# Routed experts in 128-slot blocks from a bf16 copy of the weights in DRAM, each expert loaded once

## The chip, the cores and the metric

The kernel runs on all 8 cores of one Trainium2 chip. Every core works on one sequence of the batch and on its own copy of the inputs; nothing is exchanged. The metric is the device time of the slowest core in microseconds (us).

## The reference, cut to what matters

```python
x = x + attention(layernorm(x), Wq, Wk, Wv)       # causal, one head of width 1024; x: (8, 2048, 1024)
h = layernorm(x)
shared = (silu(h @ shared_gate.T) * (h @ shared_up.T)) @ shared_down.T    # inner width 2048
probs = sigmoid(h @ router_w.T)                    # 8 experts
scores, indices = top_k(probs, 2); scores /= scores.sum(-1)
w[t, e] = the score of token t for expert e, zero elsewhere
routed = sum_e w[:, e] * ((silu(h @ gate_w[e]) * (h @ up_w[e])) @ down_w[e])
x = x + shared + routed
```

One expert is 3 x 1024 x 2048 = 6.29 million weights, f32 in DRAM. A core has 2048 tokens and so 4096 pairs of token and expert. With the reference's inputs the pairs spread evenly: on every core each expert gets between 448 and 577 of them.

## The kernel before

It is written by hand for the five engines, each with its own program (`sync_program`, `gpsimd_program`, `tensor_program`, `vector_program`, `scalar_program`), ordered by semaphores. PE is TensorE, DVE VectorE, ACT ScalarE, POOL GpSimd, SP the engine that only issues DMAs and waits. Names that begin with `t_`, `s_`, `v_` are semaphores that TensorE, ScalarE and VectorE raise.

**Attention.** `x` goes into `R2` (f32, all 2048 tokens). Layernorm, transposes into `XQ` (feature by token), then K, V and Q from `wk`, `wv`, `wq`, which POOL loads with a cast from f32 to bf16 (only POOL's DMAs cast here); `wq` waits for the last K product. Causal scores, softmax and weighted values run tile by tile (16 query tiles of 128). The second layernorm's rows go to the DRAM tensor `x2` and, transposed, to `XQ`.

**Routing.** L506 gives the logits. The DVE program then runs `route_choose` (the two largest per token) ahead of its first product, and `route_place` after product 4. Every instruction of these goes through `chain`, which raises `v_rt` and waits for it. `tri` and `ones` are 128x128 constants for two small matmuls that turn the choice into ranks. 32 indirect DMAs write token and score of each slot to the table `tab` in DRAM, which comes back as `tabS`.

**Shared expert.** Two halves of 1024 tokens. `unit` computes 128 inner features of 512 tokens: 8 matmuls 128x512 for gate (L515), 8 for up (L519), with the weights as stationary and the tokens as moving operand, so the product is already feature by token. ScalarE takes the silu (L895), VectorE multiplies (L748). `down` then makes 16 matmuls per 128 tokens and 512 columns (L527). POOL streams the weights with the cast.

**Routed experts.** Slots are sorted by expert and each expert's share is padded to blocks of `BS` = 512: `NBLK` = (2*2048 + 8*511)//512 = 15 blocks, always all of them. A block loads its expert's weights whole, f32 to bf16 (8 gate/up groups of 1 MB bf16, in the six `slots`, and 4 parts of `dw`, into `VBUF` or a part of `R2` by turns), though neighbouring blocks mostly have the same expert. `gather_block` fetches 4 x 128 rows of `x2`, `transpose_block` (L539) turns them, then 16 units, then 8 `down` of 16 matmuls. VectorE scales by the score (L782) and POOL adds the rows to `out` in DRAM with an indirect, accumulating DMA (L388), one per 128 rows.

Of the kernel before, what the change touches and what calls it, by code (L numbers as in the profile page):

```python
# [7 lines left out]
I32 = mybir.dt.int32  # L8
AF = mybir.ActivationFunctionType
# [11 lines left out]
BS = 512  # L21
NBLK = (2 * S + NE * (BS - 1)) // BS
SUB = BS // 128
NSUB = NBLK * SUB
NSLOT = NBLK * BS
NKB = S // BS
NC_L8, NC_L16, NC_KB, NC_BI = 0, 64, 320, 320 + NKB
NCONST = NC_BI + NBLK
RT_SEL, RT_SLOT, RT_ALL = 12, 36, 39
# [12 lines left out]
def build_program():  # L42
# [6 lines left out]
    sgu_d = nc.dram_tensor("sgu", [8, 128, 4096], F32, kind="ExternalInput").ap()  # L49
    sdw_d = nc.dram_tensor("sdw", [4, 128, 4096], F32, kind="ExternalInput").ap()  # L50
    gu_d = [nc.dram_tensor("gu%d" % g, [NE, 128, 4096], F32, kind="ExternalInput").ap()
            for g in range(8)]
    dw_d = [nc.dram_tensor("dw%d" % k, [NE, 128, 4096], F32, kind="ExternalInput").ap()
            for k in range(4)]
# [13 lines left out]
    R2 = nc.alloc_sbuf_tensor("R2", [128, NTT, D], F32)  # L68
    XQ = nc.alloc_sbuf_tensor("XQ", [128, NHC, S], BF16)
    KBUF = nc.alloc_sbuf_tensor("KBUF", [128, 16384], BF16)  # L70
    VBUF = nc.alloc_sbuf_tensor("VBUF", [128, 16384], BF16)
    WBUF = nc.alloc_sbuf_tensor("WBUF", [128, 8192], BF16)
    sS = nc.alloc_sbuf_tensor("sS", [128, 5760], BF16)
    sP = nc.alloc_sbuf_tensor("sP", [128, 2, S], BF16)
    sPT = nc.alloc_sbuf_tensor("sPT", [128, 8, 128], BF16)
    xlntm = nc.alloc_sbuf_tensor("xlntm", [128, 2, D], BF16)
    gscr = nc.alloc_sbuf_tensor("gscr", [128, 2, 512], BF16)
    ident = nc.alloc_sbuf_tensor("identsb", [128, 128], BF16)
    dmask = nc.alloc_sbuf_tensor("dmasksb", [128, 128], BF16)
    rwTs = nc.alloc_sbuf_tensor("rwTs", [128, NHC, NE], BF16)  # L80
    rbias = nc.alloc_sbuf_tensor("rbiassb", [128, NE], F32)
    lgt = nc.alloc_sbuf_tensor("lgt", [128, NTT, NE], F32)
    prb = nc.alloc_sbuf_tensor("prb", [128, NTT, NE], F32)
    sel = nc.alloc_sbuf_tensor("sel", [128, NTT * NE], BF16)
# [78 lines left out]
    init_done = sem("init_done")  # L163
    sc_done = sem("sc_done")
    tab_in = sem("tab_in")
    g_in = sem("g_in")
    out_init = sem("out_init")
    add_done = sem("add_done")

# [823 lines left out]
```

## Time and profile before

| | us |
|---|---|
| median of 3 runs (lowest, highest) | 2572.2 (2489.29, 2572.78) |
| the profiled execution | 2511.08 |
| its span on the slowest core, which is core 1 | 2509.5 |
| spans of the eight cores | 2470.6 to 2509.5 |

All rows are of that one execution and, where nothing else is said, of core 1. A window row gives, for a stretch in us from the span's start, the busy time of each engine with its count of instructions, then the clock that the throttle granted TensorE as a share of full speed, the mean busy share of the core's 16 DMA engines (short windows can show a little over 1), and the GB/s that they moved, counted at the destination. A cast from f32 to bf16 thus reads twice the GB/s shown.

### The profile page before, as it was taken

The page shows a single profiled execution, that of the slowest core. Times are in us where ns is not written, and L with a number is a line of the kernel's source. Part 1 is how long each engine was busy: PE and PEld are TensorE (multiplying, and loading weights), DVE is VectorE, ACT ScalarE, POOL GpSimd, SP SyncE. Part 2 cuts the span into 40 slices and gives each one's busy share as a digit, 9 for nine tenths or more (in the row PEclk, how much of TensorE's full clock was granted, in tenths as well). Part 3 has the DMA queues.
Part 4 walks back from the last instruction along what each step waited for, and adds up shares of the span by engine and source line. Part 5 has one row for each costly group of instructions (what it writes and reads, how often), then busy time and mean ns, then how long its engine had stood idle before and what let it go on. Part 6 is the DMA issues. An engine that isn't in the chain of part 4 may idle for free.

```text
span 2509.5 us, 26342 instructions; the slowest of 8 cores (2470.6 to 2509.5 us)
## 1 busy us (share of the span) xinstructions
PE 2057.3 (82%) x9914; PEld 959.9 (38%) x9914; DVE 471.4 (19%) x757; ACT 457.2 (18%) x856; POOL 301.4 (12%) x366
## 2 busy tenths in 40 slices
PE   0689766755899999897897977979779798797898
PEld 0335633332334444343343433434334343343343
DVE  3100143324111112121111211112112111121111
ACT  4333434431100110111101111011111120111100
POOL 1000000002300000020120201202112022020111
PEclk9789978877888899998998989989889898898999
DMA  9010100002951456989989889898898998988985
GB/s 215 2 24 11 34 22 17 14 20 30 108 74 59 77 86 146 175 138 151 159 142 172 139 152 164 143 172 144 138 179 143 161 153 138 178 145 152 164 139 96
DMA packets 62826, 287.11 MB, mean 114 GB/s; under 512 B 16192, under 2 KB 16320, under 8 KB 37072
## 3 DMA queue, kind: packets, MB, share of 16 engines
q0 software_dynamic: 47936, 263.63, 63.7%
q1 hardware_dynamic: 14768, 21.80, 2.7%
q8 instruction: 83, 1.36, 0.2%
q14 instruction: 39, 0.32, 0.0%
HBM read 457.72 MB, written 44.92 MB: 200 GB/s over the span
## 4 chain that ended last, share of the span: by engine, by line
PE 60%; DMA 28%; issue 4%; DVE 4%; ACT 2%; POOL 0%; DVEq 0%; ACTq 0%; POOLq 0%
PE psE L527 12%; DMA VBUF<-dw 12%; DMA R<-dw 12%; PE psF L527 11%; PE psA L515 7%; PE psC L519 6%; PE psD L519 6%; PE psB L515 6%; DMA WBUF<-sgu 2%; DMA WBUF<-wk 2%; PE psC L443 2%; PE psD L443 1%; DVE R L638 1%; PE psA L459 1%; PE psA L416 1%
## 5 line engine op out<-in xcount | busy, mean ns | idle before, releaser
L895 ACT ACTIVATE gscr<-psA 128x512 bf16<-128x512 f32 x152 | 90.8, 597 | 1183.6 <-PE psA L515 1183.5
L527 PE MATMUL psE<-VBUF,KBUF 128*128 128x512 bf16 x768 | 195.6, 413 | 97.6 <-DMA VBUF<-dw 95.4
L527 PE MATMUL psE<-R,KBUF 128*128 128x512 bf16 x448 | 116.7, 420 | 94.7 <-DMA R<-dw 94.7
L388 POOL DMA_INDIRECT out<-R,tabS x60 | 95.1, 1585 | 786.1 <-DVE R L782 468.7
L748 DVE TENSOR_TENSOR KBUF<-gscr,psC 128x512 bf16<-128x512 bf16 x152 | 104.5, 688 | 451.6 <-PE psC L519 416.9
L748 DVE TENSOR_TENSOR KBUF<-gscr,psD 128x512 bf16<-128x512 bf16 x152 | 104.5, 688 | 436.4 <-PE psD L519 415.6
L527 PE MATMUL psF<-VBUF,KBUF 128*128 128x512 bf16 x768 | 179.7, 389 | 0.0
L895 ACT ACTIVATE gscr<-psB 128x512 bf16<-128x512 f32 x152 | 90.8, 597 | 453.3 <-PE psB L515 435.1
L527 PEld LDWEIGHTS psE<-VBUF,KBUF 128*128 128x128 bf16 x768 | 79.7, 105 | 204.5 <-issue 140.0
L782 DVE TENSOR_SCALAR R<-psE,tabS 128x512 f32<-128x512 f32 x60 | 45.1, 751 | 432.9 <-PE psE L527 432.9
L527 PEld LDWEIGHTS psF<-VBUF,KBUF 128*128 128x128 bf16 x768 | 76.6, 100 | 95.2 <-issue 19.7
L515 PE MATMUL psA<-XQ,WBUF 128*128 128x512 bf16 x256 | 76.1, 452 | 39.2 <-DMA WBUF<-sgu 26.4
L527 PEld LDWEIGHTS psE<-R,KBUF 128*128 128x128 bf16 x448 | 47.0, 106 | 158.7 <-issue 116.2
L527 PE MATMUL psF<-R,KBUF 128*128 128x512 bf16 x448 | 101.3, 379 | 0.0
L402 PE MATMUL psG<-identsb,xlntm 128*128 128x128 bf16 x64 | 11.0, 267 | 96.2 <-DMA WBUF<-wk 54.2
L360 POOL DMA_DIRECT2D XQ<-gu x80 | 49.6, 619 | 305.5 <-PE psD L519 297.9
L519 PE MATMUL psC<-sS,XQ 128*128 128x512 bf16 x336 | 79.4, 379 | 0.0
L515 PE MATMUL psA<-sS,XQ 128*128 128x512 bf16 x336 | 79.4, 379 | 0.0
L519 PE MATMUL psD<-sS,XQ 128*128 128x512 bf16 x336 | 79.4, 379 | 0.0
L515 PE MATMUL psB<-sS,XQ 128*128 128x512 bf16 x336 | 79.4, 379 | 0.0
L443 PE MATMUL psC<-VBUF,sPT 128*128 128x512 bf16 x136 | 60.6, 446 | 21.0 <-ACT sPT L832 21.0
L782 DVE TENSOR_SCALAR R<-psF,tabS 128x512 f32<-128x512 f32 x60 | 45.1, 751 | 161.4 <-PE psF L527 161.4
(209 smaller groups left out, 2643.1 us busy)
## 6 DMA issues: line engine op xcount, KB each, us to landing
XQ<-gu POOLq DMA_DIRECT2D x80, 1024.0 KB, 37.5
WBUF<-gu POOLq DMA_DIRECT2D x40, 1024.0 KB, 37.6
VBUF<-dw POOLq DMA_DIRECT2D x32, 1024.0 KB
R<-dw POOLq DMA_DIRECT2D x28, 1024.0 KB, 33.0
WBUF<-sgu POOLq DMA_DIRECT2D x16, 1024.0 KB, 10.4
R<-x SPq DMA_DIRECT2D x4, 2048.0 KB, 24.0
out<-R SPq DMA_DIRECT2D x16, 512.0 KB, 2.6
x<-xlntm SPq DMA_DIRECT2D x16, 256.0 KB, 2.0
```

What stands on the lines that cost most here:

```text
L360: eng.dma_start(out=halves(slots[r % 6]), in_=halves(src)).then_inc(w_in[r % 6], 16)
L388: eng.indirect_dma_start(out=out_d, out_offset=bass.IndirectOffsetOnAxis(ap=tabS[:, q, 0:1], axis=0), in_=y[:, q % 4, :], in_offset=None, ...
L416: mm = eng.matmul(b[:, 0:w], XQ[:, ec, qi * 128:(qi + 1) * 128], kfm[:, ec, ks * 512:ks * 512 + w], start=(ec == 0), stop=(ec == NHC - 1))
L443: mm = eng.matmul((psC, psD)[eh][:, :], sPT[:, kc % 8, :], vtm[:, kc, eh * 512:(eh + 1) * 512], start=(kc == 0), stop=(kc == qi))
L459: mm = eng.matmul(pj[g % 4][:, :], wqkv[:, d, ec * 128:(ec + 1) * 128], XQ[:, d, ts * 512:(ts + 1) * 512], start=(d == 0), stop=(d == NHC ...
L515: mm = eng.matmul((psA, psB)[u % 2][:, :], w[:, 0, hc, ic * 128:(ic + 1) * 128], moving[:, hc, :], start=(hc == 0), stop=(hc == NHC - 1))
L519: mm = eng.matmul((psC, psD)[u % 2][:, :], w[:, 1, hc, ic * 128:(ic + 1) * 128], moving[:, hc, :], start=(hc == 0), stop=(hc == NHC - 1))
L527: mm = eng.matmul((psE, psF)[n % 2][:, :], a[:, i, tt * 128:(tt + 1) * 128], w[:, i, hh * 512:(hh + 1) * 512], start=(i == 0), stop=(i == ...
L638: eng.scalar_tensor_tensor(R2[:, qi, eh * 512:(eh + 1) * 512], (psC, psD)[eh][:, :], qst[:, 3, qi:qi + 1], R2[:, qi, eh * 512:(eh + 1) * 512],
L748: eng.tensor_tensor(dst, gscr[:, u % 2, :], (psC, psD)[u % 2][:, :], op=ALU.mult).then_inc(v_mul, 1)
L782: eng.tensor_scalar(y[:, q % 4, hh * 512:(hh + 1) * 512], (psE, psF)[n % 2][:, :], tabS[:, q, 1:2].bitcast(F32), None, op0=ALU.mult).then_ ...
L895: eng.activation(gscr[:, u % 2, :], (psA, psB)[u % 2][:, :], AF.Silu).then_inc(s_silu, 1)
```

## The change

**Weights.** The host packs each expert (the shared one is number 8) into 8 chunks of [128, 6144] f32: 256 columns of gate, the same 256 of up, and the 256 rows of down that belong to them. 72 POOL DMAs without a wait between them cast all nine experts, DRAM to DRAM, into `wb` (bf16). SP, whose DMAs can't cast, then loads chunks of `wb` into `wring`, two buffers of one expert each (98,304 bytes per partition and buffer). The whole of SBUF is one tensor `arena`; attention's tensors lie where the ring will be.

**Blocks.** `BS` = 128, so `NBLK` = (4096 + 8*127)//128 = 39 blocks, always all of them. From the reference's inputs 34 to 37 of them are filled on a core, and each expert has 4 or 5. VectorE computes for each block which buffer holds its expert (`pints`) and which load, if any, follows it (`lints`). A load that isn't needed is skipped by a condition on the DMA. A load for the next expert goes out when the last block of the one before has left the buffer, and the first expert's waits for all casts.

**Steps.** Shared and routed work have one form: 55 tiles of 128 tokens (16 shared, 39 routed), 8 steps each. Step k: `gate_up` (8 matmuls 128x512, tokens stationary, weights moving), `transpose_h` of step k-2 (2 transposes), `down` of step k-3 (4 matmuls 128x512). ScalarE takes the silu of 256 columns and copies the transposed product, VectorE multiplies 256 columns.

```diff
-BS = 512
+NCH = 8
+CH = 6144
+BS = 128
@@ gpsimd_program
         eng.wait_ge(t_kv, 32)
         eng.dma_start(out=wqkv[:, :, :],
                       in_=wq_d.rearrange("(c p) e -> p c e", p=128)).then_inc(wq_in, 16)
-        load_shared(0, 0)
-        load_shared(0, 1)
+        for e in [NE] + list(range(NE)):
+            for c in range(NCH):
+                eng.dma_start(out=wb_d[c][e, :, :], in_=w_d[c][e, :, :]
+                              ).then_inc(cast_done[0 if e == NE else 1], 16)
+
+        eng.wait_ge(t_pt, pair_no["p", NTT - 1, n_pairs(NTT - 1) - 1] + 1)
+        eng.dma_start(out=tri, in_=tri_d).then_inc(tri_in, 16)
         eng.wait_ge(v_rt, RT_SLOT)
@@ sync_program
+        def before_first(c):
+            if c == 0:
+                eng.wait_ge(cast_done[1], 16 * NCH * NE)
+            if c == 5:
+                store_out(NTT - 1)
+                eng.wait_ge(t_gu, NCH * NTT)
+            elif c < 5:
+                for tt in range(3 * c, 3 * c + 3):
+                    store_out(tt)
...
+        load_expert(0, before_first)
+        load_expert(1, lambda c: eng.wait_ge(t_dn, NCH * (NTT - 1) + c + 1))
+        for blk in range(NBLK - 2):
+            load_expert(blk + 2, lambda c: eng.wait_ge(t_dn, NCH * (NTT + blk) + c + 1))
@@ tensor_program
+        def moving(k, off, use):
+            tile, c = k // NCH, k % NCH
+            if tile < NTT:
+                return use(wring[:, 0, c, off:off + 512])
+            v = bass.RuntimeValue.of_register_unchecked(base[tile - NTT], min_val=0,
+                                                        max_val=B1 // 2) * 2
+            at_byte = 2 * (c * CH + off)
+            mm = use(arena[:, bass.ds(v + at_byte, 1024)].bitcast(BF16))
...
+        for k in range(NSTEP + 3):
+            if k < NSTEP:
+                gate_up(k)
+            if 2 <= k < NSTEP + 2:
+                transpose_h(k - 2)
+            if k >= 3:
+                down(k - 3)
+            if k == 4:
+                eng.wait_ge(v_rt, RT_SEL)
+                eng.matmul(psH[:, 0:128], tri, sel, start=True, stop=True)
+                eng.matmul(psH[:, 128:256], ones, sel, start=True, stop=True).then_inc(t_rk, 1)
+            if k == NCH:
+                eng.wait_ge(v_rt, RT_ALL)
+                eng.load(base[0:20], pints[0:1, 0:20])
+                eng.load(base[20:NBLK], pints[0:1, 20:NBLK])
@@ vector_program
         def route_choose():
             eng.wait_ge(s_sig, 1)
-            eng.wait_ge(init_done, 48)
+            eng.wait_ge(rc_in, 32)
+            eng.wait_ge(tri_in, 16)
+            chain(eng.memset(ones, 1.0))
...
+        route_choose()
+        for k in range(NSTEP + 3):
+            if k < NSTEP:
+                product(k)
+            if k % NCH == 2 and k > NCH:
+                evacuate(k // NCH - 1)
+            if k == 5:
+                route_place()
+                route_blocks()
```

In `gate_up`, step k waits for product k-3 (`v_mul`), since three PSUM banks take turns. The routing is 77 chained instructions in place of 39.

Where instructions move, shown at three places (in the rows `arena` is any tensor of the change in SBUF, and what stands in brackets is what the instruction waits for).

POOL's program before, from the constants to the first writes of the table: `tri` comes early, and behind `wq` come two groups of the shared expert.

```order
L312 DMA trisb<-tri 128x128
L313 DMA WBUF<-wk 128x8x1024
L315 DMA sS<-wv 128x4x1024
L317 DMA sP<-wv 128x4x1024
L319 DMA x<-zero 16x8192
L321 DMA WBUF<-wq 128x8x1024 [waits t_kv]
L288 DMA WBUF<-sgu 128x4096 [waits t_q] x2
L293 DMA tab<-tabsb,slot 7680x2 [waits v_rt,init_done]
L293 DMA tab<-tabsb,slot 7680x2 x5
```

POOL's program in the change, from `wv` to the first gather: the 72 casts stand behind `wq` with no wait of their own, and `tri`, the 32 writes of the table and the gathers now stand behind the casts.

```order
L389 DMA arena<-wv 128x4x1024
L391 DMA arena<-wv 128x4x1024
L393 DMA x<-zero 16x8192
L395 DMA arena<-wq 128x8x1024 [waits t_kv]
L399 DMA wb<-w 48x16384 x72
L403 DMA arena<-tri 128x128 [waits t_pt]
L408 DMA tab<-arena 4992x2 [waits v_rt,init_done]
L408 DMA tab<-arena 4992x2 x31
L377 DMA arena<-x,arena 128x1024 [waits v_rt,tab_in,x2_out,pad_done]
```

Moved: `tri` from the first constants to behind the last cast; new: 226 MB read and 113 MB written in one run of POOL's queue.

VectorE before, the start of `route_choose`: it waits for `s_sig` and for constants that SP loads on its own queue.

```order
L692 TENSOR_REDUCE rst<-prb 128x16 [waits s_sig,init_done]
L693 TENSOR_TENSOR KBUF<-prb,rst 128x128 [waits v_rt]
L684 TENSOR_TENSOR KBUF<-KBUF 128x1024 [waits v_rt]
L686 TENSOR_REDUCE KBUF<-KBUF 128x128 [waits v_rt]
L687 SCALAR_TENSOR_TENSOR KBUF<-KBUF 128x128 [waits v_rt]
L696 SCALAR_TENSOR_TENSOR KBUF<-KBUF,prb 128x128 [waits v_rt]
```

VectorE in the change, the same place: the first instruction waits for `tri_in` too. 18 more of the chain follow without another engine's semaphore, then product 0 (L830).

```order
L750 MEMSET arena 128x128 [waits s_sig,rc_in,tri_in]
L739 TENSOR_REDUCE arena<-arena 128x16 [waits v_rt]
L740 TENSOR_TENSOR arena<-arena 128x128 [waits v_rt]
L741 TENSOR_TENSOR arena<-arena 128x128 [waits v_rt]
L742 TENSOR_REDUCE arena<-arena 128x16 [waits v_rt]
L743 TENSOR_TENSOR arena<-arena 128x128 [waits v_rt]
```

Moved: the constants' load is now waited for from POOL's queue as well; the products stand behind the routing as before.

TensorE before, the start of a routed block: 8 gate and 8 up matmuls per unit, with addresses fixed in the program.

```order
L515 MATMUL psA<-sS,WBUF 128x512 [waits s_x,w_in0,s_silu,v_mul]
L515 MATMUL psA<-sS,WBUF 128x512 x7
L519 MATMUL psC<-sS,WBUF 128x512 x8
L515 MATMUL psB<-sS,WBUF 128x512 [waits s_silu,v_mul]
L515 MATMUL psB<-sS,WBUF 128x512 x7
L519 MATMUL psD<-sS,WBUF 128x512 x8
L515 MATMUL psA<-sS,WBUF 128x512 [waits w_in1,s_silu,v_mul]
L515 MATMUL psA<-sS,WBUF 128x512 x7
```

TensorE in the change, in a routed block, from the `transpose_h` of one step to the first `gate_up` matmul of the next: each 128x512 matmul on the ring has an instruction ahead of it that computes its address in a register.

```order
L585 MATMUL psF<-arena 128x128 [waits v_mul,s_ht]
L585 MATMUL psF<-arena 128x128
L600 REGISTER_ALU [waits s_ht]
L600 MATMUL psD<-arena 128x512
L600 REGISTER_ALU
L600 MATMUL psE<-arena 128x512
L600 REGISTER_ALU
L600 MATMUL psD<-arena 128x512
L600 REGISTER_ALU
L600 MATMUL psE<-arena 128x512
L576 REGISTER_ALU [waits we_in1_1,v_mul]
L576 MATMUL psC<-arena 128x512
```

What moved: gate and up are one accumulation of 512 columns, the down products stand among them, and the 3,744 matmuls 5,280 such matmuls the 3,744 of the routed blocks have that instruction; the 1,536 of the shared expert have none.

## Rows read from the trace of the kernel before

**Rows 1.** The page's 40 slices: busy tenths of TensorE and of the DMA engines.

```profile
PE   0689766755899999897897977979779798797898
...
DMA  9010100002951456989989889898898998988985
```

**Rows 2.** Windows of the stages: attention, shared expert, routed blocks.

```profile
302.00:566.00 264.00, 174.99 (x958) 84.75 (x956) 95.03 (x206) 98.84 (x256) 0.00 (x0) 0.80 0.07 22
566.00:984.00 418.00, 376.01 (x1569) 161.26 (x1570) 84.75 (x136) 44.87 (x71) 48.37 (x60) 0.88 0.52 82
984.00:2510.00 1526.00, 1308.64 (x6218) 597.47 (x6216) 255.84 (x361) 196.25 (x296) 244.64 (x290) 0.92 0.89 151
```

**Rows 3.** The chain that ended last: start us, us, what.

```profile
1014.92 36.83 DMA VBUF<-dw
1052.10 6.38 PE psE L527 x16
1058.48 3.45 PE psF L527 x16
...
1111.44 44.39 DMA R<-dw
```

**Rows 4.** A window inside a block, between accumulating DMAs.

```profile
1114.00:1144.00 30.00, 26.01 (x143) 12.56 (x141) 5.41 (x8) 7.96 (x11) 2.12 (x4) 0.98 1.01 169
```

**Rows 5.** Windows of core 0: its first shared-expert load, from 292 us.

```profile
296.00:298.00 2.00, 2.00 (x14) 1.54 (x12) 0.58 (x2) 0.00 (x0) 0.00 (x0) 0.50 1.09 229
...
300.00:302.00 2.00, 1.28 (x7) 0.62 (x7) 1.16 (x4) 1.07 (x5) 0.00 (x0) 0.88 0.98 172
```

**Rows 6.** Windows of core 1, the same load, from 295 us.

```profile
300.00:302.00 2.00, 2.00 (x10) 1.15 (x9) 0.87 (x4) 0.00 (x0) 0.00 (x0) 0.50 1.00 176
...
306.00:308.00 2.00, 0.77 (x5) 0.14 (x3) 1.89 (x3) 0.00 (x0) 0.00 (x0) 1.00 1.00 205
```

**Rows 7.** Timeline of POOL: start us, us, engine line op out<-in.

```profile
175.59 0.93 POOL L321 DMA_DIRECT2D WBUF<-wq  x1 [167.79 <-PE psD L459]
```

**Rows 8.** DMA issues: out<-in engine op xcount, KB, us to landing.

```profile
XQ<-gu POOLq DMA_DIRECT2D x80, 1024.0 KB, 37.5
...
out<-R SPq DMA_DIRECT2D x16, 512.0 KB, 2.6
...
WBUF<-wq POOLq DMA_DIRECT2D x1, 2048.0 KB, 17.2
...
sP<-wv POOLq DMA_DIRECT2D x1, 1024.0 KB, 58.7
...
x<-zero POOLq DMA_DIRECT2D x1, 256.0 KB, 59.3
```

**Rows 9.** Line 360, POOL's sequencer: min/median/max ns.

```profile
L360 POOLq ALU_OP  x30: 32/32/49, 913.6 to 2335.6; - x30
```

**Rows 10.** Line 349, a register loaded from SBUF: min/median/max ns.

```profile
L349 POOLq TENSOR_LOAD <-eblki x15: 285/291/498, 900.3 to 905.0; - x15
```

**Rows 11.** Timeline of TensorE: the transposes of a block.

```profile
1137.74 0.61 PE L539 MATMUL psG<-identsb,sP 128*128 128x128 bf16 x8
1138.19 0.61 PE L539 MATMUL psH<-identsb,sP 128*128 128x128 bf16 x8
```

**Rows 12.** Timeline of VectorE: two neighbours of the routing's chain.

```profile
572.71 0.29 DVE L696 SCALAR_TENSOR_TENSOR KBUF<-KBUF,prb 128x128 f32<-128x128 f32 x1
573.10 0.29 DVE L698 TENSOR_REDUCE rst<-KBUF 128x16 f32<-128x128 f32 x1
```

**Rows 13.** Core 1 in the shared expert's first `down`.

```profile
735.00:800.00 65.00, 63.99 (x245) 26.37 (x244) 10.32 (x15) 0.10 (x1) 0.53 (x1) 0.81 0.24 73
```

**Rows 14.** Core 2 in the same stretch.

```profile
735.00:800.00 65.00, 65.00 (x302) 29.45 (x301) 13.07 (x19) 2.32 (x4) 0.00 (x0) 1.00 0.22 74
```

**Rows 15.** The page's costliest groups: ScalarE's silu.

```profile
L895 ACT ACTIVATE gscr<-psA 128x512 bf16<-128x512 f32 x152 | 90.8, 597 | 1183.6 <-PE psA L515 1183.5
```

**Rows 16.** Timeline of POOL: the last accumulating DMA.

```profile
2501.14 1.55 POOL L388 DMA_INDIRECT out<-R,tabS  x1 [5.35 <-DVE R L782]
```

More of the change, by code:

```diff
@@ L1 @@
+import math
 import numpy as np
@@ new lines, in build_program @@
+    slot = in_u(2 * NTT).bitcast(I32).rearrange("p (k a) -> p k a", k=2)
+    bt1, bt2 = [in_u(NBLK * NE).rearrange("p (b e) -> p b e", b=NBLK) for _ in range(2)]
+    bev = in_u(2 * NBLK * 4).rearrange("p (b e) -> p b e", e=4)
+    od, kk, fl, le, nx = [in_u(NBLK) for _ in range(5)]
+    par = in_u(2 * NBLK)
+    pev = in_u(2 * NBLK)
+    e8 = rconst[:, NC_E8:NC_E8 + NE]
+    eid = rconst[:, NC_ID:NC_ID + NE]
+    l8 = rconst[:, NC_L8:NC_L8 + 64].rearrange("p (a b) -> p a b", a=NE)
+    kbs = rconst[:, NC_KB:NC_KB + NKB]
@@ L311, in gpsimd_program @@
                       in_=rwT_d.rearrange("(c p) e -> p c e", p=128)).then_inc(c_in, 16)
-        eng.dma_start(out=tri[:, :], in_=tri_d).then_inc(c_in, 16)
         eng.dma_start(out=wqkv[:, :, :],
@@ new lines, in gate_up @@
+        def gate_up(k):
+            tile, c = k // NCH, k % NCH
+            blk = tile - NTT
+            if tile == 0:
+                eng.wait_ge(ws_in[c], 16)
+            elif blk >= 0:
+                if c == 0:
+                    eng.wait_ge(s_x, blk + 1)
+                eng.wait_ge(we_in[blk % 2][c], 16 * (blk // 2 + 1))
+            if k >= 3:
+                eng.wait_ge(v_mul, k - 2)
+            for hc in range(NHC):
+                x = XQ[:, hc, tile * 128:(tile + 1) * 128] if blk < 0 else xT[:, blk % 2, hc, :]
+                mm = moving(k, hc * 512, lambda w: eng.matmul(
+                    psGU[k % 3][:, :], x, w, start=(hc == 0), stop=(hc == NHC - 1)))
+            mm.then_inc(t_gu, 1)
@@ new lines, in transpose_h, with down @@
+        def transpose_h(k):
+            eng.wait_ge(v_mul, k + 1)
+            if k >= 1:
+                eng.wait_ge(s_ht, k)
+            for j in range(2):
+                mm = eng.transpose(hps[:, k % 2, j * 128:(j + 1) * 128],
+                                   sil[:, k % 3, j * 128:(j + 1) * 128], ident[:, :])
+            mm.then_inc(t_ht, 1)
+        def down(k):
+            tile, c = k // NCH, k % NCH
+            eng.wait_ge(s_ht, k + 1)
+            if c == 0 and tile == 0:
+                eng.wait_ge(v_lg, 1)
+            if c == 0 and tile >= 1:
+                eng.wait_ge(v_y, y_written(tile - 1))
+                if tile > NTT:
+                    eng.wait_ge(s_y, tile - NTT)
+            for j in range(2):
+                for hh in range(2):
+                    mm = moving(k, 4096 + j * 1024 + hh * 512, lambda w: eng.matmul(
+                        psY[hh][:, :], hT[:, k % 2, j * 128:(j + 1) * 128], w,
+                        start=(c == 0 and j == 0), stop=(c == NCH - 1 and j == 1)))
+            if tile >= NTT and c == NCH - 1:
+                v = bass.RuntimeValue.of_register_unchecked(base[tile - NTT], min_val=0,
+                                                            max_val=B1 // 2)
+                eng.free_register(eng.lower_val(v * 2))
+                eng.free_register(base[tile - NTT])
+            mm.then_inc(t_dn, 1)
```

696 lines of the change are left out of this document (322 added, 374 removed).

## The prediction

> **What bounds the kernel now.** I read the page's 40 slices first [rows 1]. TensorE is busy everywhere, but from the sixteenth slice on the DMA engines are at 8 or 9 tenths as well, so the busy share alone doesn't say which of them sets the pace. The windows by stage [rows 2] give the sizes: attention ends near 566 us, the shared expert takes 418 us, the 15 routed blocks 1526 us, that is 101.7 us each, with the DMA share at 0.89. The chain of waits [rows 3] decides it. In every block a stretch of 37 to 44 us belongs to the landing of the down weights, and only the last part of the block to TensorE's 3.45 us per 16 matmuls. A block computes 384 matmuls of 512 columns at 3.45/16 = 0.216 us, which is 83 us; its weights are 25.2 MB of f32, and at the 169 GB/s (338 GB/s read) of a window of weight loads alone [rows 4] they take 74 us, to which gathers and additions come. So the routed stage stands between two limits, and the loads decide its last wait. TensorE's 5,760 routed matmuls (1242 us) lie close under it.
>
> **What the change takes away.** 39 blocks of 128 slots hold 4,992 slots, where 15 of 512 hold 7,680. The matmuls per slot stay the same, so 3,744 are left, 2,016 fewer: 435 us of TensorE at 0.216. Added are 2 transposes in each of the 440 steps (55 tiles x 8); the 8 transposes per 128 slots go from 480 to 312. Eight transposes start 0.45 us after the eight before them [rows 11], 0.056 each. Each expert has 4 or 5 blocks of about 22 us, so its successor's 12.6 MB have 88 us or more to arrive, and at 338 GB/s they need 37. The waits of [rows 3] therefore go in the routed stage.
>
> **When the casts end.** This carries the forecast. POOL issues `wq` at 175.6 us [rows 7], and it lands 17.2 us later [rows 8], at 193. The casts follow in the same queue with no wait. Nine experts of 6.29 million weights are 226.5 MB read and 113.2 MB written, all in DRAM; in the same time SP stores `x2` (4.2 MB) and reads the shared copy (12.6 MB). Sum 356.5 MB. What rate? Two cores show that they share the memory. Core 0 loads at 229 GB/s while core 1 hasn't begun, and at 172 when both load [rows 5]; core 1 has 176 then, and 205 once core 0 is done [rows 6]. Since the cast reads twice what it writes, both together take some 340 GB/s each from DRAM, the same as [rows 4]. No row has reads and writes of DRAM mixed at full rate. One bound counts only reads (239 MB at 338: 707 us, casts end at 900). The other counts all bytes and takes a tenth off for the mixing (1172 us, end at 1365). I take all bytes at 338, because what two cores compete for is the memory, and the writes go to it as well: 1055 us, end at 1248.
>
> The Trainium skill, HBM Reference, Specifications, gives about 358 GB/s per core when both cores of a pair run. The trace is 6% under it. By that figure the casts would end at 193 + 996 = 1189 and the sum below would be 59 us lower.
>
> **Who waits for the casts.** The first expert's load does, by its own wait. But `tri`, 32 KB, stands behind the 72 casts in POOL's queue too. That the queue is served in order shows in the landings: a load of 1 MB, which takes 6 us alone at 169 GB/s, lands 37.5 us after its issue when others stand ahead, and `x` from `zero`, issued behind `wv`, lands last [rows 8]. VectorE's `route_choose` waits for `tri` ahead of product 0, and step 3 waits for product 0. So TensorE finishes attention at about 566 us, does three `gate_up`, and stands until 1250. All attention work is under this cover, with any delay that the casts cause in the `x2` stores: it would have to last 680 us to cost anything. If the cover is gone, the shared expert runs beside the casts (rival below).
>
> The Trainium skill, DMA: Bandwidth & Descriptors, Queues, rings and completion order, says that each engine takes a ring's descriptors in ring order; by this `tri` can't overtake. It also says that an engine goes round between the queues, so an SP load of `tri` would have passed. The rows agree with the first.
>
> **From the casts' end to the end.**
> - Landing of `tri`, 2 us (like 2.6 for a store [rows 8]). 19 chained instructions, 13 of them 0.39 apart [rows 12], 6 shorter, near 0.3: 7 us. A start at the lower of the clock's two levels, 2 us.
> - After product 5, 58 chained instructions at about 0.3: 17.4 us. TensorE has three steps of its own meanwhile (8 us), so 9 us are exposed.
> - At step 8 TensorE loads 39 registers. One costs 0.29 us on POOL [rows 10]; two instructions fetch them all, so the cost lies between 0.6 and 11.3 us; I take 6.
> - 440 steps of 12 x 0.216 + 2 x 0.056 = 2.70 us: 1188 us; 312 transposes of rows, 17 us; less three `gate_up` done before, 5 us. Beside it, in a step, ScalarE has one silu of half the 512 columns that take 0.60 us [rows 15] and one copy, so it fits.
> - The address instruction ahead of each matmul: 32 ns on POOL's sequencer [rows 9]. A transpose with its weight load passes in 56 ns, and 56 + 32 is far below 216: nothing. That is the bound from below; a matmul with a register's address has no row, and if it took the spacing to 0.27 it would cost 200 us.
> - First expert: its chunk 5 lies on `R2` and may load only when tile 15 is stored. Evacuation 1.5, store 2.6 [rows 8], landing about 7: 11 us against the 5 that two steps cover. Chunks 6 and 7 come at 4.7 us against steps of 2.7. Together 10 us.
> - Last addition: as now 8 to 10 us from its issue [rows 16]; 10.
>
> Sum: 1248 + 11 + 9 + 6 + 1200 + 10 + 10 = 2494 us at the full clock.
>
> **The clock.** TensorE works 1200 us without a gap on all cores. Before, while all cores computed densely, core 2 was granted 1.00 and core 1 only 0.81 for the same 65 us [rows 13, 14]. At 0.81 a step takes 2.70/0.81 = 3.33 us, 0.63 more. The slowest core counts; between never and always I take a sixth of the steps at 0.81, nearer to core 2's row since the clock was 0.92 on core 1 over the whole routed stage with its rests [rows 2], +46 us, bounds 0 and 100 for the likeliest case. **Forecast 2540 us**, 1% over the profiled execution's 2511, which lies between the lowest (2489) and the median (2572) of the runs shown.
>
> **Rivals.**
> 1. *Writes cost the memory nothing.* The casts end at 900, 348 us earlier: about 2190 us. For it: one core alone read at 458 GB/s [rows 5], so its DMA engines are not the limit. Against it: the competition of two cores. Chance 12%.
> 2. *`tri` doesn't wait for the casts*, so the change does what it is meant to: the shared expert runs from 566 to about 940 in their cover, and only the routed blocks follow the casts. 1248 + 39 x 22.1 + 15 for first loads + 10 + the clock's 30: 2165 us. Against it the order of landings. Chance 8%.
> 3. *TensorE is slowed as soon as it is dense* (slower). Nothing now lets it rest for 1200 us. At 0.81 throughout: 2494 + 440 x 0.63 = 2771 us; it decides against the forecast from about half the steps on. For it core 1's rows, against it core 2's. Chance 12%. The Trainium skill, TensorE: Matmul & The Clock Gate, The HAM clock gate, says that dense matmuls on three cores of a die take the whole die to 13/16 of the clock. That is this rival. The trace agrees with the level (0.81) and not with the reach: core 2 of the same die kept 1.00.
> 4. *Register addresses slow the matmuls* (slower): 2540 + 200 = 2740. Chance 4%.
>
> **How the numbers follow.** The likeliest case has 64%. Its own range is 2435 (casts by the smaller figure's 59 us less, full clock) to 2700 (mixing costs a tenth, +117, and clock +100). A change of 2% is about what a measurement of this kernel can tell from none; against 2489 to 2511 that is below about 2450, or above about 2555. Of the 64, I put 8 below, 28 within and 28 above. With rivals 1 and 2 (20) below and 3 and 4 (16) above: faster 0.28, same 0.28, slower 0.44. The range from 2165 to 2740 leaves out most of rival 1 and the upper half of rivals 3 and 4.
>
> **What would show it.** A DMA share near 1 from 193 us to the casts' end, with about 108 GB/s of bf16 written; `tri` landing at 1248; TensorE idle from 570 until then; steps of 2.70 us behind it with no wait for weights except in the first routed block. Wrong would be the forecast if TensorE starts the shared expert before 600 us, if the casts end before 1150, or if a step takes over 3 us.

## The result and the profile after

The changed kernel took 2569.85 us (median of four runs, lowest 2567.4), the kernel before on the same chip 2541.11 (median of four). The ratio is 1.028, 95% interval [1.020, 1.035]: slower by nearly 3%. It isn't the quotient of the two medians: it compares 2489.3 and 2510.0 us before with 2567.4 to 2570.0 after, since two of the four runs before (2572.8 and 2572.2), one of the changed kernel (2741.47, with one die's mean granted clock at 0.76 to 0.80 and not 0.82) and such runs of the experiments below (five of the six with `tri` early) were in a slower state, and what is said of the clock holds for the others alone. The profiled execution of the changed kernel took 2567.4 us, on its slowest core, 6, a span of 2565.6. The result lies inside the range, but the forecast of 2540 lay 1.3% under the median of 2572.2 that was shown before it and 1.2% over the profiled 2511, so it called no clear change where there is one.

First the page's slices of the changed kernel, beside [rows 1].

```profile
PE   0689722233343010000149999959999999999997
...
PEclk9789966566666555555569999989999999999999
DMA  9029999999999999999702111182774572735111
GB/s 210 1 32 117 110 130 115 113 115 114 116 115 114 114 133 140 112 138 132 108 9 59 50 49 51 44 293 45 226 214 130 153 228 44 235 89 184 39 38 26
```

The two engines have changed places. From slice 4 to slice 19 the DMA engines are full. TensorE falls to 2 to 4 tenths from slice 6 and to nearly nothing from slice 14. From slice 22 it is full, but for one slice, and the DMA engines rest between bursts. The routed stage lost the weight waits of [rows 3] as intended, and what the casts cost before it was added in front. The windows of core 6 (columns as in [rows 2]) give the sizes.

```profile
315.00:900.00 585.00, 156.79 (x776) 75.49 (x788) 82.79 (x170) 94.20 (x242) 0.59 (x1) 0.64 1.00 117
...
1190.00:1250.00 60.00, 0.00 (x0) 0.00 (x0) 0.00 (x0) 0.00 (x0) 0.00 (x0) 0.50 1.00 117
1272.00:1342.00 70.00, 30.97 (x128) 13.10 (x132) 20.12 (x72) 6.53 (x19) 31.03 (x32) 0.67 0.03 8
1342.00:1670.00 328.00, 326.26 (x1668) 156.11 (x1700) 69.84 (x150) 79.26 (x243) 1.95 (x2) 1.00 0.14 51
1670.00:1720.00 50.00, 26.82 (x128) 12.21 (x129) 4.54 (x10) 8.14 (x20) 3.56 (x3) 0.89 0.96 308
1720.00:2557.00 837.00, 825.73 (x4403) 402.63 (x4490) 154.41 (x337) 257.29 (x674) 95.00 (x73) 1.00 0.45 129
```

While only casts ran, 117 GB/s were written, and the read side moves twice that. Behind 1342 the clock is 1.00 except around the first routed blocks (0.89 in the window from 1670), and of the last 837 us TensorE is busy for 826. The wait itself, in VectorE's timeline and then in TensorE's, each with the idle time and its releaser in brackets:

```profile
1265.18 0.17 DVE L750 MEMSET arena<- 128x128 bf16 x1 [346.64 <-DMA arena<-tri]
```

```profile
1272.67 0.37 PE L585 MATMUL psF<-arena 128*128 128x128 bf16 x2 [278.76 <-DVE arena L830]
```

VectorE stood 347 us for `tri` and ran `route_choose` in 7.5. The landings of the small transfers say why (engine, size, us to landing).

```profile
arena<-rconst SPq DMA_DIRECT2D x1, 69.5 KB, 148.8
arena<-tri POOLq DMA_DIRECT2D x1, 32.0 KB, 446.9
arena<-tokid SPq DMA_DIRECT2D x1, 8.0 KB, 180.7
```

```profile
x<-arena SPq DMA_DIRECT2D x16, 256.0 KB, 40.3
```

That is the page's median of the 16 stores of `x2`: 40 us each beside the casts, where a store of twice its size took 2.6 before [rows 8]. The 181 us of `tokid` (8 KB) are not its own price alone, since it stands behind three chunks of the shared expert and `rconst` in SP's queue; it lands 32 us after `rconst`. That stretched attention from 566 us to 918, in the cover of the casts. Last, the waits that are left from 1260 us on (us in total, times, longest), in which the first row is the wait for `tri`.

```profile
PE psF L585 <- DVE arena L830: 278.8, 1, 278.8
PE psF L585 <- ACT arena L970: 21.0, 1, 21.0
PE psB L576 <- DMA arena<-wb: 14.5, 4, 8.4
PE psF L585 <- issue: 14.4, 1, 14.4
PE psA L576 <- DMA arena<-wb: 6.1, 3, 3.0
PE psC L576 <- DMA arena<-wb: 4.9, 3, 2.6
PE psA L576 <- issue: 1.8, 1, 1.8
```

### The profile page after: what moved, and what is told of

Same layout as the page of the kernel before. It is cut to its first block, busy times and chain, and to the rows that moved or that the text cites. A ratio compares the mean times of both kernels' runs of the same rounds, so it can differ in the third digit from the quotient of the medians.

```text
span 2565.6 us, 31247 instructions; the slowest of 8 cores (2536.8 to 2565.6 us)
## 1 busy us (share of the span) xinstructions
PE 1586.1 (62%) x8455; PEld 786.9 (31%) x8610; DVE 382.4 (15%) x834; ACT 571.1 (22%) x1450; POOL 175.7 (7%) x196
## 3 DMA queue, kind: packets, MB, share of 16 engines
q0 software_dynamic: 19040, 150.63, 47.6%
q1 hardware_dynamic: 22448, 134.91, 15.5%
## 4 chain that ended last, share of the span: by engine, by line
PE 53%; DMA 24%; another core or an unknown queue 17%; issue 2%; DVE 1%; ACT 1%; SPq 0%; POOL 0%; POOLq 0%; DVEq 0%; ACTq 0%
DMA x<-arena 20%; PE psA L576 10%; PE psB L576 10%; PE psC L576 9%; PE psE L600 8%; PE psD L600 7%; DMA arena<-wk 2%; PE psF L585 2%; DMA arena<-wb 2%; PE psA L498 1%; PE psG L615 1%; PE psB L498 1%; PE psA L522 1%; PE psD L522 1%
## 5 line engine op out<-in xcount | busy, mean ns | idle before, releaser
L600 PE MATMUL psE<-arena 128*128 (+1 forms) x880 | 335.2, 381 | 3.9 <-DVE arena L830 1.0
L585 PE MATMUL psF<-arena 128*128 128x128 bf16 x880 | 121.5, 220 | 314.2 <-DVE arena L830 278.8
L600 PE MATMUL psD<-arena 128*128 (+1 forms) x827 | 314.9, 381 | 0.0
L576 PE MATMUL psB<-arena 128*128 (+1 forms) x1157 | 280.2, 385 | 50.5 <-DMA arena<-wb 49.5
L576 PE MATMUL psC<-arena 128*128 (+1 forms) x1135 | 274.9, 381 | 37.1 <-DMA arena<-wb 35.4
L576 PE MATMUL psA<-arena 128*128 (+1 forms) x1154 | 283.5, 386 | 9.3 <-DMA arena<-wb 6.1
L970 ACT COPY arena<-psF 128x256 bf16<-128x256 bf16 x440 | 161.6, 367 | 297.8 <-PE psF L585 294.7
L576 PEld LDWEIGHTS psB<-arena 128*128 128x128 bf16 x1176 | 115.6, 99 | 189.6 <-issue 57.9
L576 PEld LDWEIGHTS psC<-arena 128*128 128x128 bf16 x1168 | 113.9, 98 | 172.2 <-issue 39.5
L576 PEld LDWEIGHTS psA<-arena 128*128 128x128 bf16 x1176 | 116.0, 99 | 149.2 <-issue 18.6
L830 DVE TENSOR_TENSOR arena<-arena,psB 128x256 bf16<-128x256 bf16 x147 | 61.9, 421 | 361.7 <-ACT arena L964 357.1
L830 DVE TENSOR_TENSOR arena<-arena,psA 128x256 bf16<-128x256 bf16 x147 | 61.9, 421 | 335.0 <-ACT arena L964 325.5
L830 DVE TENSOR_TENSOR arena<-arena,psC 128x256 bf16<-128x256 bf16 x146 | 61.5, 421 | 322.6 <-ACT arena L964 316.6
## 6 DMA issues: line engine op xcount, KB each, us to landing
x<-arena SPq DMA_DIRECT2D x16, 256.0 KB, 40.3
```

What stands on the lines that cost most here:

```text
L576: mm = moving(k, hc * 512, lambda w: eng.matmul(psGU[k % 3][:, :], x, w, start=(hc == 0), stop=(hc == NHC - 1)))
L585: mm = eng.transpose(hps[:, k % 2, j * 128:(j + 1) * 128], sil[:, k % 3, j * 128:(j + 1) * 128], ident[:, :])
L600: mm = moving(k, 4096 + j * 1024 + hh * 512, lambda w: eng.matmul(psY[hh][:, :], hT[:, k % 2, j * 128:(j + 1) * 128], w, start=(c == 0 and ...
L830: eng.tensor_tensor(sil[:, k % 3, :], sil[:, k % 3, :], psGU[k % 3][:, 256:512], op=ALU.mult).then_inc(v_mul, 1)
L970: eng.copy(hT[:, k % 2, :], hps[:, k % 2, :]).then_inc(s_ht, 1)
```

## The experiments

All edits are of the changed kernel. Ratios are to the kernel before, run in turns on the same chip; it took 2531 us (median) beside the first four kernels and 2493 to 2497 beside the others. The changed kernel's own time hardly moved between chips (2566 to 2570), so edits are compared with it in us.

### `tri` early

```diff
+        eng.dma_start(out=tri_e, in_=tri_d).then_inc(tri_in, 16)   # gpsimd_program, before wk
...
-        eng.wait_ge(t_pt, pair_no["p", NTT - 1, n_pairs(NTT - 1) - 1] + 1)
-        eng.dma_start(out=tri, in_=tri_d).then_inc(tri_in, 16)
```

> The changed kernel with one thing undone: the 32 KB of tri are loaded among the first constants into spare columns and copied by VectorE to their place before the router's step, so that only the experts' loads, the scatters and the gathers stand behind the casts. Theory (the queue position of tri, and not the casts' bytes as such, holds TensorE idle from 918 to 1273 us): tri's semaphore is there at once, the shared expert starts at about 930 and ends near 1300 us, still beside the casts; the first routed step comes about 40 to 60 us after the casts' end at 1265, then some 900 us of routed work as in the changed kernel: 2190 to 2230 us in all, about 350 less than the changed kernel's 2568. Rival (the shared expert, moved under the casts, is starved by their traffic: its chunks, its stores and the resets of the output crawl as the stores of x2 did): shared ends no earlier than about 1500, total 2400 or more. Rival (the load of the first expert, behind the casts in any case, is the real gate): TensorE's idle stretch only moves behind the shared stage and the total stays above 2500.

Measured: 2550.65 us, from one run, so without an interval; 17 less than the changed kernel, not 350. The waits of TensorE from 880 to 1500 us:

```profile
PE psB L576 <- DMA arena<-wb: 143.5, 3, 83.5
PE psF L585 <- DVE arena L832: 106.4, 1, 106.4
...
PE psC L576 <- DMA arena<-wb: 67.8, 2, 35.1
```

SP's queue in order of time shows where they come from (start, us that the group spans):

```profile
922.60 1.62 SPq L295 DMA_DIRECT2D arena<-wb  x3
...
924.79 0.65 SPq L340 DMA_DIRECT2D arena<-tokid  x1
925.54 1.83 SPq L295 DMA_DIRECT2D arena<-wb  x3
927.47 326.78 SPq L290 DMA_DIRECT2D x<-arena  x2
1289.93 0.35 SPq L295 DMA_DIRECT2D arena<-wb  x1
```

The theory fell as I had put it, and the first rival holds: the shared expert ends near 1650 (forecast by the rival: 1500 or later) and the total is over 2400. Nothing waits for `tri` any more, and still the shared expert can't run at its pace beside the casts. Its chunks come one per 35 to 39 us where a step takes 2.7, `tokid` holds `route_choose` until 1108, and the store of `x2` behind them all lands 327 us after its issue, so the shared expert's last chunk goes out at 1290. It reaches full pace at 1312, when the casts are over, and the total is what it was. The queue position was one gate; behind it stood a second of the same height, the pace of everything on SP beside the casts.

### Short rows, and a middle size

```diff
-    wb_d = [nc.dram_tensor("wb%d" % c, [NE + 1, 128, CH], BF16, kind="Internal").ap()
+    wb_d = [nc.dram_tensor("wb%d" % c, [NE + 1, 128, 3, 2112], BF16, kind="Internal").ap()
...
-                eng.dma_start(out=wb_d[c][e, :, :], in_=w_d[c][e, :, :]
+                eng.dma_start(out=wb_d[c][e, :, :, 0:2048], in_=rows(w_d[c][e, :, :])
```

`rows` splits 6144 values into 3 x 2048. The second kernel is the same with one piece of 6144 in a row of 6208.

> The changed kernel with the bf16 copy laid out in pieces of 2048 values with a gap between them, so that one descriptor of a cast reads 8 KB and writes 4 KB and not 64 and 32 KB; the same bytes are moved, tri stays last in its queue. Theory (the engines take turns between queues, one descriptor each, so a 4 KB row of x2 waits for a whole cast row): the 16 stores of x2 fall from 40 us each to about 5 us, attention ends near 600 instead of 918 us, the casts still end at 1250 to 1270, and the total stays at about 2565 us, since all that is gained lies in front of the wait for tri. Rival (the stores are slow for the share of bandwidth that the casts leave, whatever the size of a descriptor): they stay at about 40 us. Rival (short descriptors cost the casts themselves): casts end after 1300 and the total rises by the same.

> The changed kernel, tri last, with pieces of 6144 values: one descriptor of a cast reads 24 KB and writes 12 KB, between the 64 and 32 KB of the changed kernel (a store of x2 in 40.3 us) and the 8 and 4 KB of the short ones (13.0 us). Each engine carries 8 rows of a store. Theory (each row waits for one descriptor of the cast queue, and that takes a fixed part and a part by its bytes): with the two points, 8 turns of 1.14 + 0.061 us a KB read, so 8 x 2.6 = 21 us a store; attention then ends near 700 us and the total stays within 2550 to 2610. Rival (only long descriptors that the engine has to split are slow, or the share of bandwidth decides): 13 or 40 us again.

Measured: short rows 2596 us (ratio 1.025 [1.022, 1.028]), middle rows 2571.9 (one run). The page's row of the stores of `x2`, first with short rows, then with middle ones:

```profile
x<-arena SPq DMA_DIRECT2D x16, 256.0 KB, 13.0
```

```profile
x<-arena SPq DMA_DIRECT2D x16, 256.0 KB, 21.8
```

40.3, 21.8 and 13.0 us at 64, 24 and 8 KB read per descriptor: with 128 rows over 16 engines, 8 rows of 5.0, 2.7 and 1.6 us each. The middle one had been forecast at 21 from the other two. Attention ended near 642 us with it (forecast 700). The packets of the software queue agree with the sizes: 19,040, 24,800 and 43,232, so 72 casts have 48, 128 and 384 each. So what a store on SP's queue waits for hangs on the bytes in one descriptor of the cast queue. It does not hang on the share of bandwidth: the engines were full in all three, and the cast's bytes the same. That each row waits for exactly one descriptor is my reading and not shown. A cast takes 1072/72 = 14.9 us, so one of its descriptors occupies its engine for some 5.0, 1.9 and 0.6 us (an estimate from the three counts): this gives the whole of a row's wait at 64 KB, and leaves 0.8 to 1.0 us over at the two shorter sizes. With short rows attention ends near 560 us, and TensorE then waits 694 instead of 279 us: nothing is gained, as forecast. The casts themselves end 25 us later (`tri` at 1290 against 1265), which is the whole loss of 26 us; that rival was right in a small way.

### Both edits

> Both edits: tri early and short descriptors. Theory: attention ends near 600, the shared expert runs 610 to about 1000 us beside the casts, TensorE then waits for the casts' end at about 1265 plus scatter, table and gather, and the routed stage takes 900: 2180 to 2210 us, at most 30 less than with tri early alone, since the casts' end is then the bound of both. Rival (attention's stretch was a cost of its own): well below 2150 us.

Measured: 2296.8 us, ratio 0.907 [0.904, 0.910]. The page's slices:

```profile
PE   0669866675122999994000035899999999999997
...
DMA  9008999999999999999999958481854637262121
```

The shared expert now runs at full pace from 738 to 1062 us in the cover of the casts (its first chunks still cost waits before 738), and the only long wait behind that is the one for the first gather:

```profile
PE psG L619 <- DMA arena<-x,arena: 278.4, 1, 278.4
```

Neither edit alone was worth more than 17 us, both together 270. It is some 90 us above the upper end of the theory. The casts end at 1300 us (SP leaves their wait at 1301.1), then 37 us go by for table and gather and some 55 in the first routed blocks, whose chunks of `wb` queue among 16 stores of `out`.

### Half the casts

```diff
-        for e in [NE] + list(range(NE)):
+        for e in [NE] + list(range(4)):
```

Experts 4 to 7 are then computed with the weights of expert 3, so this kernel leaves out part of the work of the casts and its output is not the reference's; only its time is of use.

> The changed kernel casts the shared expert and experts 0 to 3 only; experts 4 to 7 are computed with expert 3's weights, so four ninths of the cast bytes are left out and nothing else. Theory (the shared stage starts when the casts end, and the casts' time goes with all bytes, 39.6 MB a expert at about 340 GB/s): casts end near 193 + 5 x 119 = 790 us; attention, whose last x2 stores are then free, ends at about 850 to 880, the shared stage starts there, and the total is about 2165 to 2200 us. Rival (a fixed cost, a clock or the routed stage itself makes the time): a fall of less than 200 us. Rival (only reads count): the casts would end no earlier than in proportion too, so this run only prices the bytes; the slope is what it gives.

Measured: 2132 us, ratio 0.843 [0.840, 0.845]. The windows of its slowest core:

```profile
193.00:780.00 587.00, 240.45 (x1405) 136.83 (x1421) 84.72 (x180) 129.18 (x275) 4.17 (x9) 0.71 1.00 115
780.00:790.00 10.00, 4.38 (x21) 2.05 (x22) 1.15 (x4) 3.67 (x8) 0.00 (x0) 0.59 0.16 60
```

The casts end at 781 us: 588 us for five experts, 118 each, where the changed kernel has 1072 for nine, 119 each. The cost goes with the number of casts, and so with their bytes; reads and writes fall together here, so it doesn't tell one from the other. Attention, held up by its stores until the casts end, ends at 821, and `tri` now lands 12 us after its issue. The total is some 436 us lower, somewhat more than forecast; here attention and no longer the end of the casts sets the start of the shared expert.

### Casts streamed by expert

From here on `tri` early and short rows are in every kernel but the last pair. The core of the edit:

```diff
+        cast(4 * NCH)                      # shared expert, experts 0 to 2; then the scatters
...
+        cast(NCH)                          # expert 3; then table and gathers 0 and 1
+        cast(NCH)                          # expert 4
...
                 gather(blk + 2)
+                cast((6 * (blk + 1) + 4) // 5 - (6 * blk + 4) // 5)
@@ load_expert(n)
+            if n % 4 == 1 and (n - 1) // 4 + 1 < NE:
+                eng.wait_ge(cast_done[(n - 1) // 4 + 1], 16 * NCH)
```

> The kernel with tri early and short descriptors, and the casts no longer in one piece: one semaphore for each expert's copy, the load for block n waits only for the expert that block n can need (every expert has at least four blocks here), and GpSimd issues the shared expert and experts 0 to 2 first, then the scatters of the slot table, expert 3, the first two gathers, expert 4, and the last 24 chunks one or two a block beside blocks 0 to 19. Theory (what is left in the kernel with both edits is TensorE's 278 us wait from the end of the shared stage at 1060 to the casts' end plus the first gather at 1338): the wait goes to under 50 us, the routed stage of 39 blocks takes its 900 to 955 us from about 1070, 1990 to 2060 us in all. Rival (casts in GpSimd's queue beside the routed work hold up the gathers and the adds as they held up the stores of x2): blocks 0 to 19 take 30 us or more each and the total is 2150 or more. Rival (the wait was for something else than the casts, the table or the gather for instance): no change from 2297.

Measured: 2207 to 2229 us, ratio 0.887 [0.881, 0.893]. The windows of two neighbouring stretches of its routed stage:

```profile
1180.00:1250.00 70.00, 66.21 (x355) 32.09 (x359) 12.69 (x28) 20.80 (x55) 9.93 (x9) 1.00 0.83 142
1250.00:1320.00 70.00, 27.57 (x97) 11.30 (x100) 3.28 (x7) 5.58 (x14) 3.93 (x4) 0.66 0.93 196
```

Theory and rival each had a part. The wait for all casts is gone and the routed stage starts at 1066, but TensorE waits for `wb` in five stretches of 38 to 62 us, 236 us in all behind 1066. This order of casts, and that of the two kernels below, counts on at least four blocks for each expert, which these inputs give. I took the DMA engines to be oversubscribed there and moved casts forward:

```diff
-        cast(NCH)
+        cast(2 * NCH)
...
-                cast((6 * (blk + 1) + 4) // 5 - (6 * blk + 4) // 5)
+                cast((8 * (blk + 1) + 10) // 11 - (8 * blk + 10) // 11)
```

> As the streamed kernel, but experts 4 and 5 are both cast right behind the first two gathers, where the trace of the streamed kernel has the DMA engines 72% busy from 850 to 1066 us, and only 16 chunks, of experts 6 and 7, are spread over blocks 0 to 21. Theory (its routed blocks are bound by the DMA engines from 1066 to 1790, since a switch of expert reads 12.6 MB beside seven or eight casts of 15 us each): with 4 casts an expert and not 6 the stalls at the first five switches shrink from 50 to 60 us each to about 20 to 30, and the total falls from 2207 to 2070 to 2130 us. Rival (the load of an expert comes only two blocks ahead of its use, so it stalls there whatever is cast beside it): total within 2180 to 2220. Rival (the third gather now waits behind two experts' casts and TensorE with it): block 2 starts after 1200 and nothing is gained.

Measured: 2185 us, ratio 0.876 [0.872, 0.880], so some 30 of the 100 us expected; the first rival's figure. Two windows tell why. First one of the changed kernel, the load of one expert with nothing beside it; then the same in this kernel.

```profile
1798.00:1838.00 40.00, 39.74 (x216) 19.56 (x220) 7.40 (x16) 12.62 (x33) 5.16 (x4) 1.00 1.00 316
```

```profile
1268.00:1356.00 88.00, 56.65 (x272) 25.95 (x270) 9.09 (x20) 16.17 (x41) 8.26 (x8) 0.83 1.00 211
```

12.6 MB take 40 us alone, and 88 beside a few casts, with TensorE stalled. Yet behind each such burst the DMA share is 0.2 for two blocks, so they aren't oversubscribed over an expert's 4 or 5 blocks. The deadline is what is wrong. Block n waits for load n, and each chunk of load n goes out when the same step of block n-2 is done, so each real load has two blocks, 44 us. The weights that it brings are first needed an expert later.

### Each block waits for its own expert's load

```diff
-                eng.wait_ge(we_in[blk % 2][c], 16 * (blk // 2 + 1))
+                n = max(blk - 3, 0)
+                eng.wait_ge(we_in[n % 6][c], 16 * (n // 6 + 1))
```

> As the kernel with the casts streamed earlier, with one wait changed: TensorE's block n waited for load n, which brings the next expert's weights and is issued when block n-2 is done, so each real load had two blocks (44 us) to land, though its weights are first needed an expert later. Now block n waits for load n-3 (blocks 0 to 3 for load 0), which is enough where every expert has at least four blocks; the semaphores are six sets and not two. Theory (the stalls of 30 to 55 us at each change of expert are that wait: a load lands in 44 us alone and in 75 to 90 beside casts): they vanish, blocks 1 to 38 run at 22 us, the waits for weights are left only in block 0, and the total falls by 100 to 150 us to 2030 to 2080. Rival (the DMA engines are simply oversubscribed there): the stalls stay, a few blocks later, and the total is 2150 or more.

Measured: 2057.7 us, ratio 0.825 [0.821, 0.829], 128 us less than the kernel that it is compared with and 510 less than the changed kernel. All waits of TensorE behind 1060 us:

```profile
PE psA L595 <- DMA arena<-wb: 51.9, 4, 42.4
PE psB L595 <- DMA arena<-wb: 32.6, 2, 24.6
PE psC L595 <- DMA arena<-wb: 22.3, 2, 12.1
PE psD L619 <- DVE arena L863: 3.9, 2, 2.7
```

Of these 107 us for `wb`, 79 lie before 1160, in block 0. Behind it 27 us are left, in four waits, where the kernel before this edit had 125. So the stalls at the changes of expert were for the most part the wait and not the bandwidth.

### Late scatters, and the changed kernel once more

Since the two dies of the changed kernel differ by 24 us at one clock, I looked for the cause.

```profile
die 0 (median of its cores): 2539.5 us, clock 0.821
die 1 (median of its cores): 2563.2 us, clock 0.820
```

ScalarE's timeline, core 4 of the changed kernel:

```profile
1326.96 0.38 ACT L964 ACTIVATE arena<-psB 128x256 bf16<-128x256 f32 x1 [19.68 <-remote]
```

Core 0 has the same silu at 1313, and cores 0 to 3 have no such wait. The edit is one wait ahead of the scatters:

```diff
         eng.wait_ge(v_rt, RT_SLOT)
+        eng.wait_ge(t_dn, 24)
```

> The changed kernel with GpSimd's 32 scatters of the slot table held back until 24 products of the shared expert are done, some 60 us later, in the middle of its steps. In the changed kernel ScalarE stands for 17 to 23 us at its silu of step 9 on the four cores of one die and on no core of the other, while GpSimd issues those scatters. Theory (the scatters cause it): the stall of about 20 us moves to about 1385 us with the scatters and the four cores of one die are again 20 us longer; total 2560 to 2575. Rival (it belongs to the place in ScalarE's program, the first pass of that code or the routing beside it): it stays at 1315 to 1338 us and the scatters run without one. Rival (it comes only where both meet): no stall, total about 2545.

> The changed kernel once more, unchanged, on the chip of this call, for its time beside the kernel before and for the spread of its own figures: 2555 to 2575 us, tri landing at 1255 to 1275 us, the stall of ScalarE on one die of the two.

Measured: late scatters 2578 us (one run, 3 us over its range), once more 2566.4 and 2569.9, with `tri` landing at 1262 us. Core 4 with late scatters:

```profile
1398.03 0.38 ACT L965 ACTIVATE arena<-psB 128x256 bf16<-128x256 f32 x1 [24.89 <-remote]
```

Another 9 us were lost just before. The stall moved with the scatters (1353 to 1392 us there), and in both kernels it is on cores 4 to 7 alone; in the run with middle rows it was on cores 0 to 3 alone. The place in the program isn't the cause, the scatters are. The kernel before has the same thing, smaller: on core 1, in the stretch of its own scatters (602 to 682 us), ScalarE has three waits of 5.5 to 7.1 us with nothing on the core to release it.

```profile
ACT gscr L895 <- remote: 18.2, 3, 7.1
```

With `tri` early alone, and in the streamed kernels, TensorE had little to do while the scatters went out (busy 4 to 7 of 39 us) and the wait doesn't show on any core. So it appears where scatters meet running steps. By what path they hold ScalarE stays open: the profile names no releaser on the core. On two cores of the run with late scatters part of the gap has no releaser of any kind.

## Why the prediction had the gate right and missed the slowdown

It was right that the casts' end releases `tri` and that `tri` releases TensorE. The step that failed is the sum from there on: 2494 us at the full clock against 2567 measured, 73 short. ScalarE's stall was not in it at all, and the casts' end, the steps and the weights of the first routed blocks were taken too small. The clock term of 46 us measured 0 and hid most of the gap. What was left, 27 us, is the difference between no clear change and a kernel that is 2.8% slower.

The measured ledger on core 6, in the order of the prediction's sum.

| step | forecast | measured |
|---|---|---|
| casts' end and landing of `tri` | 1250 | 1265.2 |
| `route_choose` and restart | 9 | 7.5 |
| VectorE's chain behind product 5 | 9 | 14.4 |
| 39 register loads | 6 | 1.8 |
| ScalarE's stall at the scatters, and 1 us behind it | - | 22.0 |
| steps and transposes, waits taken out | 1200 | 1216 |
| waits for weights, first routed blocks | 10 | 25.5 |
| last matmul to the end | 10 | 14.5 |
| clock | 46 | 0 |
| sum | 2540 | 2567 |

**When the casts end** came out within 17 us. Priced by all bytes, reads and writes, 356.5 MB in 1072 us are 333 GB/s, 1.6% under the 338 that I took from loads. Rival 1 (writes cost nothing, end at 900) is out, and so is the mixing loss of a tenth. Why the writes cost is not shown. I had put it on the memory that two cores share. But the DMA share was 1.00 all the while, and in windows with casts alone the pace hangs on the descriptor: 117, 111 and 107 GB/s written with 64, 24 and 8 KB read per descriptor (1190 to 1250 us, and 1000 to 1200 in the two other kernels), three times that of all bytes. At least part of the limit then lies with the DMA engines; no run had one core of a pair cast alone, which would tell. The Trainium skill, HBM Reference, Specifications, would have had them end at 1189; this run measures 1265. In the window with casts alone the trace comes to 351 GB/s, 2% under that page's figure, and over the whole stretch to 333.

**Who waits for the casts** was right about `tri`, and its cover too. Attention ran 350 us longer under it than I had worked out and cost nothing, as against the bound of 680. But the size of that stretch I had left open, and **rival 2 was mis-priced**: I gave 2165 us if `tri` doesn't wait, on the assumption that the shared expert would run at its pace beside the casts. With `tri` early the time was 2551. The rival had taken the DMA share of SP's loads from their bytes, when beside descriptors of 64 KB a transfer of 128 rows takes 35 to 40 us whatever its bytes. With both edits the time was 2297, still 132 us over its figure. The Trainium skill, DMA: Bandwidth & Descriptors, Queues, rings and completion order, says that a DMA engine goes round between its queues, and that it drains a whole packet of descriptors from one before it switches. I had read that as an SP load passing freely. The three sizes of descriptor show a price of 1.6 to 5.0 us per row; whether a turn is one descriptor or several they don't tell.

**The sum at the full clock** was 73 us short. The clock term gave back 46 of these, so the forecast is near the measured time in part by luck. The largest misses are ScalarE's stall (22), the steps (16; after each wait the first products run at half clock, 3.57 us for eight matmuls and not 1.89), the first routed blocks (15.5) and the casts (15). The stall was at nothing in the sum, though the trace of before has 18 us of such waits beside its scatters (above). For the routed blocks I had given each expert's load 88 us or more, four blocks, when by the program's waits it has two, 44 us; at 40 us a load that was just enough, but in blocks 0 and 1 it wasn't. Register addresses cost nothing visible: a step is 2.70 us in the shared expert, whose 1,536 matmuls of 512 columns have none, and in the routed blocks, whose 3,744 have one each. Rival 4 is out.

**The clock.** I took a sixth of the steps at 0.81. From 1342 to 2557 us of the profiled execution the granted clock was 1.00 but for the windows with a wait, on all eight cores. The level 0.81 of [rows 13] didn't come up in 1200 us of dense matmuls on all cores, so rival 3 is out for this execution. By the rule of the Trainium skill, TensorE: Matmul & The Clock Gate, The HAM clock gate, all cores should have been at 13/16; this trace disagrees.

**The sign.** The forecast was 1% over the profiled execution of before and 1% under the median of its runs, and that median is not what the comparison uses; against its 2489 to 2510 the forecast would have been 1.6% slower. It came out 27 us higher still. The chance of slower, 0.44, was the largest of the three, so the chances leaned the right way where the forecast did not say it. By the prediction's own terms the upper end of the likeliest case is 2494 + 117 + 100 = 2711 and not 2700; nothing hangs on it.

## What to carry to other kernels

A small constant behind a long row of transfers in the same queue is a gate; but before pricing its removal, ask at what pace all the other queues run beside those transfers, and look for the second gate of the same height. Where two queues share the engines, the rows that each engine carries of the short transfer, times the time of one long descriptor, are the least that it costs (8 x 5.0 = 40 us here at 64 KB; with shorter descriptors 7 to 8 us more than this product), and cutting the descriptors is worth something only together with the wait that hides it. For prefetches, take the deadline from the wait that the consumer makes and not from when it needs the data: here that wait was worth 128 us.

## What the runs showed of the hardware that I had not expected

- Beside casts whose descriptors read 64, 24 and 8 KB, a store of 128 rows on another queue takes 40.3, 21.8 and 13.0 us.
- DRAM to DRAM casts on all eight cores at once, with SP's stores and loads beside them, move 333 GB/s a core of reads and writes together. With descriptors of 8 KB read, `tri` behind them lands 25 us later than with those of 64 KB.
- Where 32 indirect scatters by GpSimd met running steps of the changed kernel, ScalarE stood for 17 to 23 us on the four cores of one die, and on the other die not at all.
- In the profiled execution the granted clock stayed at 1.00 with TensorE dense on all eight cores for over 800 us.
